# Strassen's seven products for gate and up in chunks 3 to 10 of a feed-forward stage

## The reference, cut to what matters

```python
x = x + xattn0(layernorm(x), ctx)
x = x + ffn0(layernorm(x))          # this stage
x = x + xattn1(layernorm(x), ctx)
x = x + ffn1(layernorm(x))

def ffn0(h):                        # h: 1024 tokens x 512
    gate = silu(h @ w_gate.T + b_gate)      # 1376 wide
    up = h @ w_up.T + b_up                  # 1376 wide
    return (gate * up) @ w_down.T + b_down  # 512 wide
```

## Time and profile before

| what | value |
|---|---|
| time, median of 3 runs | 1677.07 us (1676.98 to 1678.69) |
| time of the profiled execution | 1678.61 us |
| its span, first to last instruction | 1676.7 us |
| TensorE busy | 1664.0 us, 99% of the span |
| VectorE busy | 868.3 us, 52% |
| GpSimd busy | 689.0 us, 41% |
| ScalarE busy | 666.3 us, 40% |
| share of TensorE in the chain that ended last | 95% |

### The profile page before, as it was taken

How to read it: one execution, slowest core, us unless ns; L and a number is a source line. 1 busy time by engine, 2 the same in 40 slices (tenths; PEclk the granted TensorE clock), 3 DMA queues, 4 the chain that set the end, 5 groups by cost and what they waited for, 6 DMA issues and landing times.

```text
span 1676.7 us, 25806 instructions
## 1 busy us (share of the span) xinstructions
PE 1664.0 (99%) x9496; PEld 1444.7 (86%) x9496; DVE 868.3 (52%) x1436; ACT 666.3 (40%) x1795; POOL 689.0 (41%) x505
## 2 busy tenths in 40 slices
PE   9999999999999999999999999999999999999999
PEld 8888888988888888888978887888888888888887
DVE  6543344344443344433463343876656755665775
ACT  6432233222332233222333212565546655554553
POOL 4622343324422343324335333645435544443445
PEclk9999999999999999999999999999999999999999
DMA  6110110111010110101001111011110110000011
GB/s 209 54 54 28 53 52 26 41 40 53 25 53 28 53 53 25 53 28 53 20 20 46 55 47 59 19 58 38 32 39 32 45 51 28 30 32 26 26 51 51
DMA packets 31331, 74.98 MB, mean 45 GB/s; under 512 B 5824, under 2 KB 10560, under 8 KB 31264
## 3 DMA queue, kind: packets, MB, share of 16 engines
q1 hardware_dynamic: 31264, 74.10, 13.3%
HBM read 71.99 MB, written 2.10 MB: 44 GB/s over the span
## 4 chain that ended last, share of the span: by engine, by line
PE 95%; DVE 2%; POOL 1%; ACT 1%; issue 1%; DMA 0%; SPq 0%; DVEq 0%; ACTq 0%; POOLq 0%
PE banks L55 27%; PE banks L57 27%; PE banks L56 27%; PE banks L474 3%; PE banks L1567 3%; PE banks L457 3%; PE banks L466 2%; PE banks L1574 1%; PE banks L207 0%; DMA x_q<-in_ctxT 0%; DVE resid L1286 0%; POOL rstd L179 0%; DVE stats L166 0%; PE banks L520 0%; DVE resid L828 0%
## 5 line engine op out<-in xcount | busy, mean ns | idle before, releaser
L954 POOL TENSOR_TENSOR x_probs<-x_probs,x_inv 128x512 f32<-128x512 f32 x64 | 66.7, 1042 | 447.1 <-DVE x_inv L796 447.1
L2031 POOL TENSOR_TENSOR g_swapped<-g_swapped,rawB 128x512 f32<-128x512 f32 x80 | 103.3, 1294 | 171.7 <-ACT g_swapped L1712 171.7
L638 ACT COPY x_pT<-banks 128x512 f32<-128x512 f32 x64 | 37.5, 587 | 334.6 <-PE banks L466 334.6
L55 PE MATMUL banks<-wtV_hi,cT_lo 128*128 128x256 f32 x512 | 145.2, 284 | 0.0
L57 PE MATMUL banks<-wtV_hi,cT_hi 128*128 128x256 f32 x512 | 144.9, 283 | 0.0
L56 PE MATMUL banks<-wtV_lo,cT_hi 128*128 128x256 f32 x512 | 144.9, 283 | 0.0
L804 DVE COPY x_k<-banks 128x512 f32<-128x512 f32 x60 | 41.5, 692 | 135.7 <-PE banks L57 135.7
L804 DVE COPY x_v<-banks 128x512 f32<-128x512 f32 x60 | 41.5, 692 | 127.9 <-PE banks L57 127.9
L55 PE MATMUL banks<-wtV_hi,g_att_lo 128*128 128x512 f32 x256 | 105.3, 412 | 0.0
L828 DVE TENSOR_TENSOR resid<-banks,resid 128x512 f32<-128x512 f32 x128 | 84.1, 686 | 39.5 <-PE banks L57 39.5
L630 ACT ACTIVATE x_probs<-x_probs,x_top 128x128 f32<-128x128 f32 x256 | 99.2, 390 | 12.1 <-DVE x_top L787 12.1
(11 more groups left out here) (243 smaller groups left out, 4921.3 us busy)
## 6 DMA issues: line engine op xcount, KB each, us to landing
rawV<-in_x_wV SPq DMA_DIRECT2D x16, 512.0 KB, 3.4
rawO<-in_x_wO SPq DMA_DIRECT2D x16, 512.0 KB, 3.6
rawO<-in_g_wQ SPq DMA_DIRECT2D x16, 512.0 KB, 3.5
rawV<-in_g_wO SPq DMA_DIRECT2D x16, 512.0 KB, 3.4
rawA<-in_x_wA SPq DMA_DIRECT2D x15, 512.0 KB, 4.6
rawB<-in_x_wB SPq DMA_DIRECT2D x15, 512.0 KB, 3.5
rawA<-in_f_gu SPq DMA_DIRECT2D x5, 512.0 KB, 3.5
rawB<-in_f_gu SPq DMA_DIRECT2D x5, 512.0 KB, 3.4
```

The source lines that it names most:

```text
L55: pe.matmul(out, w[1], x[0], start=start, stop=False)
L954: pool.tensor_tensor(probs[:, part, :], probs[:, part, :], rows, ALU.mult).then_inc(probs_ready, 1)
L2031: pool.tensor_tensor(part, part, sin[:, :].unsqueeze(1).to_broadcast([P, HB, P]), ALU.mult)\
```

## The change

From chunk 3 on, gate and up of a chunk are taken as one product of a 2 x 2 block matrix of weights (gate and up, each with two halves of the input width) with a 2 x 2 block matrix of the activations (two halves of the width, two token halves). Strassen's scheme in Winograd's form does it with seven block products of 6 matmuls in place of eight. What it needs besides:

- of the activations, four combined blocks `twist` (128 x 1024 each, high and low part). DVE makes them once, in chunks 0 to 2, from the normalised activations: eight sums and differences and low parts, and ACT casts four high parts;
- of each chunk's weights, four combined blocks of 128 x 256: POOL makes them (`combine`), ACT and POOL split three of them into new places (`dn[..., D:]`, `more`);
- sums of the products: three banks X, Y, Z are used. ACT copies X to SBUF (`first_sum`), DVE forms `second_sum`, `third_sum`, and two sums in place in PSUM; silu of the second token half is taken in place in bank Z.

TensorE's order of a chunk is now X, Y, Z, X, Y, batches 0 to 3 of `down(c - 1)`, Y, Z, batches 4 to 7. The core of the diff:

```diff
+            def seven(c, par, turn):                         # tensor
+                pe.wait_ge(gu_hi, c + 1)
+                pe.wait_ge(gu_lo, c + 1)
+                pe.wait_ge(gate_ready, 2 * c - 1)
+                half_product(m, X, a11, b11)
+                pe.wait_ge(hidden_ready, 2 * c)
+                pe.wait_ge(twist_lo, 2)
+                half_product(m, Y, s2, t2)
+                half_product(m, Z, s1, t1)
+                pe.wait_ge(copied, c - 2)
+                half_product(m, X, a12, b21, True)
+                pe.wait_ge(twist_lo, 3)
+                pe.wait_ge(sums, sums_of(c, 1))
+                half_product(m, Y, s3, t3, True)
+                down(c - 1, 1 - par, range(0, 4))
+                pe.wait_ge(twist_lo, 4)
+                pe.wait_ge(sums, sums_of(c, 2))
+                half_product(m, Y, a22, t4, True)
+                pe.wait_ge(sums, sums_of(c, 3))
+                half_product(m, Z, s4, b22, True)
+                down(c - 1, 1 - par, range(4, B))
...
+            def seven(c, par, turn):                         # scalar
+                act.wait_ge(hidden_ready, 2 * c - 1)
+                act.wait_ge(proj_ready, seq_seven(c, 0) + 1)
+                nc.scalar.copy(first_sum[0:m, :], banks[0:m, X, :]).then_inc(copied, 1)
+                act.wait_ge(proj_ready, seq_seven(c, 3) + 1)
+                nc.scalar.activation(gate[0:m, par, 0:HALF], banks[0:m, X, :], ACT.Silu, bias=bias[0:m, par, 0:1])\
+                    .then_inc(gate_ready, 1)
+                if not isinstance(c, int) or c < FULL:
+                    weights(c + 1, 1 - par, turn + par)
+                hid_high(c, par, 0)
+                act.wait_ge(sums, sums_of(c, 5))
+                nc.scalar.activation(banks[0:m, Z, :], banks[0:m, Z, :], ACT.Silu, bias=bias[0:m, par, 0:1])\
+                    .then_inc(gate_ready, 1)
+                hid_high(c, par, 1)
...
+            def seven(c, par, turn):                         # vector
+                dve.tensor_tensor(second_sum[0:m, :], y, first_sum[0:m, :], ALU.add).then_inc(sums, 1)
+                dve.tensor_tensor(third_sum[0:m, :], y, first_sum[0:m, :], ALU.add).then_inc(sums, 1)
+                dve.scalar_tensor_tensor(hidden1, z, up_bias, third_sum[0:m, :], ALU.add, ALU.add).then_inc(sums, 1)
+                for b in range(4):
+                    down_batch(c - 1, b)
+                dve.scalar_tensor_tensor(y, y, up_bias, first_sum[0:m, :], ALU.add, ALU.add).then_inc(sums, 1)
+                dve.tensor_tensor(hidden0, y, gate[0:m, par, 0:HALF], ALU.mult).then_inc(hidden_ready, 1)
+                dve.tensor_tensor(z, z, second_sum[0:m, :], ALU.add).then_inc(sums, 1)
+                down_batch(c - 1, 4)
+                dve.wait_ge(gate_ready, 2 * c + 2)
+                dve.tensor_tensor(hidden1, z, hidden1, ALU.mult).then_inc(hidden_ready, 1)
+                for b in range(5, B):
+                    down_batch(c - 1, b)
...
             body(0, 0, 0)
             dve.wait_ge(before.norm.row_added, B)
+            dve.wait_ge(before.norm.lo_ready, B)
+            summed(1, 0, 0)
+            summed(3, 0, 1)
+            summed(2, 1, 1)
+            difference(1, 3, 1, 2)
+            difference(3, 2, 3, 3)
             body(1, 1, 0)
...
+            def combine(c, par, turn):                       # gpsimd
+                pool.tensor_tensor(s3, a11, a21, ALU.subtract).then_inc(w_steps, 1)
+                pool.tensor_tensor(a21, a21, a22, ALU.add).then_inc(w_steps, 1)
+                pool.tensor_tensor(s2, a21, a11, ALU.subtract).then_inc(w_steps, 1)
+                pool.tensor_tensor(s4, a12, s2, ALU.subtract).then_inc(w_steps, 1)
```

More of the change, by code:

```diff
@@ L50, in f32, with product @@
     return ap.bitcast(F32)
[L53 to L57, removed]
+def product(pe, out, w, x, start, stop, adds=False):
+    pe.matmul(out, w[1], x[0], start=start, stop=False, skip_group_check=adds)
+    pe.matmul(out, w[0], x[1], start=False, stop=False, skip_group_check=adds)
+    return pe.matmul(out, w[0], x[0], start=False, stop=stop, skip_group_check=adds)
 def tok(b, n=1):
@@ L1143, in tensor, with down @@
         def tensor(pe):
-            def down(c, par):
+            def down(c, par, batches=range(B)):
                 pe.wait_ge(d_hi, c + 1)
                 pe.wait_ge(d_lo, c + 1)
-                for b in range(B):
+                for b in batches:
                     if b % HB == 0:
@@ L1203, in body, with half_product @@
                 down(c - 1, 1 - par)
+            def half_product(m, bank, w, x, adds=False):
+                for k in range(2):
+                    mm = product(pe, banks[0:m, bank, :], [s[:, k * m:(k + 1) * m] for s in w], [s[:, k, :] for s in x],
+                                 k == 0 and not adds, k == 1, adds)
+                mm.then_inc(proj_ready, 1)
+            def seven(c, par, turn):
+                m = rows(c)
+                w = [[s[:, n * 2 * m:(n + 1) * 2 * m] for s in gu[par]] for n in range(4)]
+                a11, a12, s1, a22 = w
+                s3, s2 = ([s[:, D + n * 2 * m:D + (n + 1) * 2 * m] for s in dn[par]] for n in range(2))
+                s4 = [s[:, 0:2 * m] for s in more[par]]
+                b11, b21, b22 = ([quarter(s, k, t) for s in xT] for k, t in ((0, 0), (1, 0), (1, 1)))
+                t1, t2, t3, t4 = twist
+                pe.wait_ge(gu_hi, c + 1)
[18 more added lines that the diff above has]
+                down(c - 1, 1 - par, range(4, B))
             first()
             body(1, 1, 0)
-            loop_rest(pe, body)
+            body(2, 0, 1)
+            loop_rest(pe, seven)
         def down_batch(pe, c, par, b):
@@ L1255, in body @@
                     cut = slice(half * HALF, (half + 1) * HALF)
+                    if c == 2 and half == 0:
+                        twist_high(2, 6)
+                    if c == 2 and half == 1:
+                        twist_high(4, 8)
                     act.wait_ge(proj_ready, seq_gu(c, half) + 1)
-                    if not isinstance(c, int) or c >= 2:
+                    if c >= 2:
                         act.wait_ge(hidden_ready, 2 * c - 2 + half - 1)
-                    nc.scalar.activation(gate[0:m, par, cut], banks[0:m, half, :], ACT.Silu,
-                                         bias=bias[0:m, par, 0:1])\
+                    nc.scalar.activation(gate[:, par, cut], banks[:, half, :], ACT.Silu, bias=bias[:, par, 0:1])\
@@ L1261, in body @@
                         .then_inc(gate_ready, 1)
-                if isinstance(c, int) and c == 0:
+                if c == 0:
                     weights_early.split_hi(act, "O", before.hooks["used_output"])
-                elif not isinstance(c, int) or c < FULL:
+                else:
                     weights(c + 1, 1 - par, turn + par)
[L1266 to L1271, removed]
@@ L1321, in body @@
                 if not isinstance(c, int) or 0 < c < FULL:
-                    weights(c + 1, 1 - par)
+                    weights(c + 1, 1 - par, turn + par)
                 for half in range(2):
```

130 lines of the change are left out of this document (118 added, 12 removed).

## The result

The changed kernel takes 1688.87 us in the median (1688.3 to 1690.26), beside 1677.26 us of the kernel before: 0.67% slower, ratio 1.0067 with a 95% interval of 1.0054 to 1.008. Forecast were 1684.5 us in a range of 1679.0 to 1690.0. The profiled execution has a span of 1687.0 us, 10.3 more than before.

The account below looks back on a forecast made before the run. The prediction took PE's matmul queue as the bound (busy 1664.0 of 1676.7 us). Removal and steady wait gave -0.3, the start +6.4, the end +1.3: +7.4 us on 1677.07, so 1684.5 us, range 1679.0 to 1690.0.

Parts of the forecast that it names:

- removal, eight products: PE's queue: six matmuls fewer in each of eight chunks, 1.36 us each, 10.9 us off.
- wait in chunks 4 to 10: Second block product waits for hidden, whose silu of Z stands behind ACT's down-weights cast: 1.52 us, seven times, +10.6 us.
- first gap: First down: PE waits for an addition behind five DVE block operations taking turns with POOL, +5.6 us.
- clock behind the gap: Rival: the granted clock falls in the first gap, up to 2.8 us more, about 1686 to 1688 us; chance 0.20.
- third chunk's weights: Between chunks 1 and 2, DVE and POOL taking turns make these weights ready about 0.8 us late.
- end of the stage: Next stage's first projection waits for POOL's low part of wtB: +1.3 us, bounds 0.7 and 2.5.
- DVE not held up: Rival at the start: no contention with POOL, 2.3 us lost, total +3.3 us; chance 0.22, shared with DVE keeping its turn.
- keeping its turn: Rival at the start: DVE hands over to its own next operation, 3.4 us lost, total +4.4 us; shared chance 0.22.
- That the wait is absent: Rival: no wait in the steady chunks, so the whole 10.9 us counts, 1673.9 to 1669.8 us; chance 0.10.
- POOL did not become the bound: Judges the rival that POOL's 256-column operations cost over 1.6 us and delay weights, 1688 us or more; chance 0.06.

Follow-up runs that it names:

- The first experiment: Changed kernel with the silu of bank Z ahead of the cast of the down weights on ACT from chunk 3 on: 1679.99 us.
- all three reorderings: Changed kernel with silu of Z first, DVE's block sums early and key weights split early: 1670.49 us, ratio 0.996 to the kernel before.
- the last kernel: Changed kernel with silu of Z first, block sums early, key weights early, plus 32 unused bytes: 1660.57 us, ratio 0.9897 to the kernel before.

## Why the prediction held, and where it was off

The sign, the places and the range were right; the sum was 3 to 4 us low (forecast +7.4, measured +10.3 in the span and +11.6 in the medians), and the median lies only 1.1 us below the upper end of the range.

| step | forecast | measured |
|---|---|---|
| removal, eight products | -10.9 | -9.1 (8 x 1.14) |
| wait in chunks 4 to 10 | +10.6 (7 x 1.52) | +10.0 (7 x 1.43) |
| first gap | +5.6 | +5.55 |
| clock behind the gap | 0, a rival with chance 0.20 | +2.1 |
| third chunk's weights | +0.8 | +1.3 |
| end of the stage | +1.3 | +1.2 |

The measured terms add up to 11.05 us, beside 10.81 by the landmarks.

- **Removal: the term that was mis-sized.** I took 0.227 us for all 42 matmuls of a chunk, from a row in which 48 of them stand in a row with xT. The same rows held the other price, 0.233 for `down`, and I didn't ask what sets the two. Five of the seven block products got the higher one, since `twist` and the last weight block lie where `f_hid` lies: 30 x 0.006 = 0.18 us a chunk. Measured are 15.34 in place of 15.12, 0.22 more; the last 0.04 were not traced. So a product fewer brings 1.14 us. The runs with unused bytes bear it out: where all tiles start alike, a product is worth 1.36 us.
- **The wait: right.** Each link was within 0.1 us of the forecast; the silu from PSUM to PSUM took 0.65 us, where I had taken 0.69 with bounds of 0.58 and 0.9. The first experiment changes this order alone, and the wait is gone.
- **The gap: right, by turn-taking.** Two rivals (DVE not held up, or keeping its turn) had 2.3 and 3.4 us here. The run in which POOL waits gives 2.12 us, the changed kernel 5.40, so the rivals are out.
- **The clock: the rival that came true.** I left it at 0.20 since no row had a gap of that length. The granted clock of 0.86 and 0.80 and the slot of 0.43 us decide it; the matmuls that fill the gap bring it back to 1.00. By the rival's own sum, up to 2.8 us, it was 2.1. The Trainium skill, page "TensorE: Matmul & The Clock Gate", section "HAM oscillation — how this bites in real kernels", had said that a gap of the array takes the clock to its lower level. The trace agrees, and I should have given it more than half: nothing in the profile spoke against it. The range had room for this rival; the sum had not.
- **Late weights and the handoff: right places, shares in part wrong.** The weights came 0.5 us later than forecast. The forecast had all ten operations of DVE beside POOL's; it did not reckon that chunk 1's additions, themselves late, would push the second five back. That is read from the order of events and was not tried alone; with the blocks early, 0.6 of the 1.1 us of this wait are left. At the end of the stage I had put all 1.3 us on the wait for wtB. It was half of that (0.6); the other half (0.56) is DVE's late additions, which the forecast had only in its lower bound.
- **The other rivals.** That the wait is absent is out (8.1 us in seven waits). POOL did not become the bound: an operation of 256 columns takes 0.73 to 0.77 us, as the line through the earlier trace rows gave. DVE gets seven operations a chunk, not five as the forecast words it; its sum of 10.5 us has all seven.

## What to carry to other kernels

An algorithm that saves matmuls pays only if the engines behind PE can give their results within the cover that is left: with one product of 1.36 us as cover, the order of two instructions on ACT cost 8.9 us, nearly all of the 9.1 that the missing matmuls saved. Put work that is done once where nobody stands behind it (7.5 us here) and, where you can't, not where DVE and POOL both read SBUF (3.8 us in the run in which POOL waits); a gap in PE can cost more than its length. And where the same matmul has two prices in a trace, ask for the cause before taking one of them: here it was where the tiles lie, and 32 unused bytes brought more (8.7 us) than the seven products with all three reorderings (7.0 us).

## What the runs showed of the hardware that I had not expected

- **The distance of the two operands' addresses.** In this kernel a matmul of 128x512 with a weight load of 128 columns has a slot of 0.227 to 0.230 us where the tiles of weights and moving operand start at the same byte modulo 128, and 0.233 where they differ by 32, 64 or 96 bytes. It isn't the whole rule: with weights of 96 columns that start alike it is 0.232. Over the kernel it is 8.7 us (1677.74 to 1669.09), 0.5%.
- **The clock can fall behind a short gap.** 2.12 us without a matmul were enough for slots of 0.43 us over the next 3.4 us, and 5.40 us for the next 4.4. The length of the gap doesn't decide alone. In the traces before and after, a gap of 1.82 us ahead of this stage left the granted clock at 1.00. At the same place the kernel before with 32 bytes behind has a gap of 1.87 us and a clock of 0.74 from 865 to 870 us, with slots of 0.43 us, while the last kernel, with 1.86 us, keeps 1.00. In the kernel without block sums the clock is 0.77 from 1055 to 1060 us; PE's last gaps before it were 1.18, 0.77 and 0.43 us.
- **Turn-taking is strict.** DVE operations of 1.18 us took up to 3.4 us beside POOL, one of POOL's for each of DVE's; neither engine got a second turn while the other waited.
